# Thinner spacing of a copy beside a chain of matrix units, earlier first loads, and a shorter mixed stage in a four-layer graph network

## The reference, cut to what matters

```
x = layernorm(x + L0(x, edges, W1, b1, W2, b2))      # two matrices, then D^-1/2 (A + I) D^-1/2
x = layernorm(x + L1(x, edges, edge_weight, ...))    # two weighted graph convolutions, hidden 128
x = layernorm(x + L2(x, src, dst, W, attn_l, attn_r, bias))   # attention over a node's incoming edges
x = layernorm(x + L3(x, src, dst, edge_attr_32, ...))         # message MLP, segment sum, update MLP
```

## Time and profile before

| what | value |
|---|---|
| median of 3 runs | 3025.3 us (3022.97 to 3028.07) |
| profiled execution, its own time | 3027.55 us |
| its span from first to last instruction | 3025.7 us |
| mean granted TensorE clock | 0.858 |
| busy share PE, DVE, ACT, POOL | 74%, 66%, 46%, 72% |
| moved by DMA | 331.63 MB, 110 GB/s over the span |

### The profile page before, as it was taken

One profiled execution on the slowest core, in us unless ns is written; L12 is line 12 of the kernel. 1 busy time (PEld: TensorE's weight loads), 2 busy tenths in 40 slices (PEclk: granted clock), 3 DMA queues, 4 the chain that ended last, 5 costly groups with the idle time before them and its releaser, 6 DMA issues.

```text
span 3025.7 us, 39571 instructions
## 1 busy us (share of the span) xinstructions
PE 2225.7 (74%) x10732; PEld 1198.3 (40%) x10732; DVE 1987.7 (66%) x3948; ACT 1382.1 (46%) x2555; POOL 2163.7 (72%) x1666
## 2 busy tenths in 40 slices
PE   2788999978888756665688859999365576666665
PEld 1333444434444435454344434444244333333332
DVE  5445788877888868666598966777688443333332
ACT  2666777755554433222344536777232232233322
POOL 7677877778776448887688858888133588888887
PEclk9989999999999979778798969999676587777777
DMA  6998422232655556555344433443366422222221
GB/s 188 290 295 226 95 57 57 57 67 63 133 122 133 123 115 152 133 128 130 76 110 108 115 86 95 102 103 90 89 162 166 98 62 54 55 56 56 56 56 25
DMA packets 619894, 331.63 MB, mean 110 GB/s; under 512 B 535780, under 2 KB 580960, under 8 KB 619677
## 3 DMA queue, kind: packets, MB, share of 16 engines
q1 hardware_dynamic: 546077, 282.42, 36.7%
q0 software_dynamic: 73600, 46.68, 9.1%
HBM read 197.17 MB, written 130.70 MB: 108 GB/s over the span
## 4 chain that ended last, share of the span: by engine, by line
POOL 50%; issue 18%; DVE 9%; DMA 9%; PE 7%; SPq 6%; ACT 1%; DVEq 0%; ACTq 0%; POOLq 0%
POOL g_row L819 34%; POOL x_with_info L826 8%; POOL out_rows L826 7%; DMA x_with_info<-wide 4%; DMA l_b<-t_x 2%; PE bank L1037 2%; SPq L697 2%; PE pair L1017 2%; DVE rT L1651 1%; DMA g_row<-t_x,gidx 1%; PE bank L946 1%; DVE x_r L1628 1%; DVE ss L1574 1%; POOL wide L910 1%; PE pair L946 1%
## 5 line engine op out<-in xcount | busy, mean ns | idle before, releaser
L819 POOL DMA_INDIRECT g_row<-t_x,gidx x600 | 809.5, 1349 | 230.7 <-issue 192.8
L1252 ACT ACTIVATE hid<-pair,b_up 128x1000 f32<-128x1000 f32 x375 | 406.2, 1083 | 44.1 <-PE pair L1018 43.3
L1038 PE MATMUL bank<-hid,w_dn 128*64 128x500 f32 x750 | 418.3, 641 | 0.0
L1037 PE MATMUL bank<-hid,w_dn 128*64 128x500 f32 x750 | 418.3, 641 | 0.0
L1017 PE MATMUL pair<-xT,w_top 64*128 64x500 f32 x550 | 321.5, 666 | 29.3 <-ACT hid L1252 26.9
L819 POOL DMA_INDIRECT g_row<-x_with_info,src_i x200 | 267.9, 1340 | 96.5 <-issue 63.6
L819 POOL DMA_INDIRECT g_row<-in_x,dst_i x200 | 262.7, 1314 | 95.2 <-issue 65.8
L1018 PE MATMUL pair<-xT,w_bot 64*128 64x500 f32 x550 | 322.4, 668 | 0.0
L819 POOL DMA_INDIRECT g_row<-t_h,gidx x200 | 260.9, 1304 | 79.7 <-issue 79.4
L826 POOL DMA_INDIRECT out_rows<-n_r,fidx x200 | 249.6, 1248 | 64.7 <-issue 60.6
L826 POOL DMA_INDIRECT x_with_info<-info_r,sidx x200 | 242.0, 1210 | 60.9 <-issue 60.9
(11 more groups left out here) (259 smaller groups left out, 5266.6 us busy)
## 6 DMA issues: line engine op xcount, KB each, us to landing
x_in<-in_x_cols SPq DMA_DIRECT2D x100, 250.0 KB, 3.1
x_with_info<-wide SPq DMA_DIRECT2D x50, 476.0 KB
wide<-in_x SPq DMA_DIRECT2D x50, 448.0 KB
out_rows<-x_r SPq DMA_DIRECT2D x100, 224.0 KB
l_k<-keep_row SPq DMA_DIRECT2D x150, 125.0 KB
l_a<-t_x SPq DMA_DIRECT2D x150, 112.0 KB
l_k<-on_row SPq DMA_DIRECT2D x50, 250.0 KB
t_x<-x_r SPq DMA_DIRECT2D x100, 112.0 KB
```

The source lines that it names most:

```text
L819: return g.indirect_dma_start(out=to, out_offset=None, in_=table, in_offset=bass.IndirectOffsetOnAxis(ap=index[:, tile:tile + 1], axis=0), ...
L1037: T.matmul(run.down[0:D, 0:CH], w_dn[a.stage][:, 0:D], hid[a.b2][:, 0, :], start=True, stop=True)
L1038: T.matmul(run.down[D:128, 0:CH], w_dn[a.stage][:, 0:D], hid[a.b2][:, 1, :], start=True, stop=True)\
L1252: A.activation(hid[a.b2][:, :, :], run.up[a.b2][:, :, 0:CH], ACT.Relu, bias=b_up[:, a.stage:a.stage + 1]).then_inc(Cn["hid"], 1)
```

## The change

Three things are edited.

1. `ext_in_slot`: behind the slots of MAIN, the remaining 42 steps of the copy stood one per slot (slots 0 to 41). They now stand three per five slots (the first in slot 1, the last in slot 69).
2. The column loads of the first three dense blocks were issued by `ask_for_columns` after all eight early steps, after a wait for DVE's scalars and after three row stores. They are now issued inside the early steps, after the fifth; `ask_for_columns` issues only those from the fourth block on.
3. `DENSE_MIXED` goes from 6 to 4, `BESIDE_D` from 74 to 76, `BESIDE_G` from 15 to 13. By `unit_order` the runs MAIN, WITH_A, WITH_C, WITH_D and WITH_G then have 163, 74, 59, 76 and 13 places. WITH_A loses two units of each dense stage and two empty places, WITH_C gains two units of each stage, WITH_D gains one of stage 1 and one of stage 2, WITH_G loses the same two.

```
-DENSE_MIXED = 6
-BESIDE_D, BESIDE_G = 74, 15
+DENSE_MIXED = 4
+BESIDE_D, BESIDE_G = 76, 13
...
-            return [] if n < 0 else range(min(EXT, EXT_EARLY + n), min(EXT, EXT_EARLY + n + 1))
+            return [] if n < 0 else range(min(EXT, EXT_EARLY + 3 * n // 5), min(EXT, EXT_EARLY + 3 * (n + 1) // 5))
...
             for b in range(EXT_EARLY):
                 ext_step(b)
+                if b == EXT_EARLY - 4:
+                    for first in range(3):
+                        sp.dma_start(x_in_c[first], t["x_cols"][first]).then_inc(Cn[f"in{first}"], 16)
             sp.wait_ge(s_c, C_DINV)
...
                             sp.wait_ge(Cn["res"], DENSE[a.b - 3].at[0] + 1)
-                        sp.dma_start(x_in_c[a.b % 3], t["x_cols"][a.b]).then_inc([Cn["in0"], Cn["in1"], Cn["in2"]][a.b % 3], 16)
+                            sp.dma_start(x_in_c[a.b % 3], t["x_cols"][a.b]).then_inc(Cn[f"in{a.b % 3}"], 16)
```

## The result

The changed kernel takes 2985.18 us (median of 4 runs, 2982.08 to 2987.25), against 3026.69 us for the kernel before in the same series: a ratio of 0.9861 with a 95% interval of 0.9844 to 0.9878, 41.5 us less. The forecast was 49 us less. The profiled execution took 2982.08 us, the fastest of the four, and its span is 2980.3, so between the two profiled spans lie 45.4 us.

The account below looks back on a forecast made before the run. POOL's chain was taken as the bound, with the scatters' start and WITH_A's length deciding ahead of level B. Scatters -28, WITH_A -26, C +3, D +4, G -2 gave -49 us: 2976 us from 3025.3, range 2962 to 2991.

Parts of the forecast that it names:

- The spacing: Copy beside slots 0 to 69: 3.55 us a slot instead of 4.89, scatters at about 332, 28 us earlier.
- (a): Rival before the scatters: the copy's last store is late at 4.1 us a slot, -12 us, 2992 us; chance 0.16.
- (d): Rival in the copy's slots: bytes don't set them, they stay at 4.89 us, 3046 us; chance 0.08 with its surroundings.
- the chain passes an own unit each three slots, 10.7 us, so it stays ahead: Own gathers: POOL takes 13.1 us a block, so its wait on PE, 29.4 us in all, goes.
- The early loads: Start of the chain: first relu at 56 us instead of 63.8, bounds 53.5 and 63.8.
- WITH_A: Units beside the iso gathers: two mixed blocks fewer save 26 us, bounds zero and 41.
- (c): Rival in WITH_A: it is paid by places, not DVE work, -41 instead of -26 us, 2961 us; chance 0.08.
- WITH_C: Beside level C: two more blocks, 18.2 us of DVE work, cost 3 us at the tail; bounds 0 and 18.
- (b): Rival in levels C and D: no usable slack, +18 + 6.4 in place of 3 + 4, about 2993 us; chance 0.13.
- WITH_D: Beside level D: two units more cost 4 us, bounds 0 and 6.4; zero by the weight-load rule.
- WITH_G: Level G: two units fewer save 2 us, bounds 0 and 4.

Follow-up runs that it names:

- z2: The changed kernel with four copy steps per five slots instead of three, the last in slot 52; 2979.7 us, 0.9853 of the kernel before.
- x4: The changed kernel with one copy step per two slots, the last in slot 83 instead of 69; 3026.0 us, 1.0004 of the kernel before.
- x2: The kernel before with only the mixed blocks at four and the runs at 76 and 13 places; 3001.4 us, 0.9927 of the kernel before.
- z4: z3 with SP asking for columns four places ahead instead of seven, in WITH_A alone; 2970.2 us, 0.9823 of the kernel before.
- z3: The changed kernel with 52 dense blocks ahead of the iso blocks, not 49, and three mixed blocks, not four; 2987.2 us, 0.9870 of the kernel before.
- y1: The changed kernel with two mixed blocks instead of four, WITH_A 66 and WITH_C 65 places; 2996.0 us, 0.9904 of the kernel before.
- y4: The changed kernel with 52 dense blocks ahead of the iso blocks, not 49, and one mixed block, not four; 2974.5 us, 0.9831 of the kernel before.

## Why the prediction was right, and where it wasn't

**The spacing.** Right in mechanism and nearly in size: 3.55 us a slot was forecast for the slow stretch and 3.57 measured; the scatters were forecast at 332 and came at 332.57. The 3.55 was a choice a little above what the bytes (3.39) and PE (3.42) gave, so that it was met to 0.02 us is luck; that the bytes set the slot down to about there is shown by z2 and x4. Rivals (a) and (d) fell in the changed kernel, but x4 shows that (a)'s wait for the copy is real one notch further.

What I had wrong is the step "the chain passes an own unit each three slots, 10.7 us, so it stays ahead". An own unit can't pass its own gather. The chain caught up with POOL and from about slot 42 was held to POOL's 13.1 us a block, so unit 70 came at 327.6, not near 305, and the copy's last store came about when POOL's last gather did, not 20 us ahead. Over slots 0 to 69 a slot took 3.91 us, just above the 3.86 from which, by the prediction's own sum, the copy is late. The term survived by luck, because the two ends happened to meet. That POOL's pace and not the 3.55 set the scatters is shown by z2, whose slots took 4.30 us and whose scatters start at 331.3.

**The early loads.** The first relu came at 54.2 (56 forecast). What I didn't say is that POOL's pace makes this worthless: alone they gave 4 us, beside the spacing nothing.

**WITH_A.** 22.4 us in the profile of the change and 25 in x2, against 26 forecast. With six mixed blocks it took 411.1 to 413.8 us in four profiles, with four, behind the same 49 dense blocks, 386.2 to 391.2 in five; the means differ by 24. DVE's busy time there fell from 347.3 to 331.4 us between unit 163 and the last one, 15.9 of the 22.4. I take the rest for idle time that left with the two empty places, which no run shows by itself. Rival (c), by places, is out. But DVE's work is not the whole of it, as the prediction had it: z4 takes 17.8 us from z3's WITH_A with the same units, by SP's queue alone, a term that the prediction didn't have. So what two mixed blocks are worth is not a constant: y1, with two fewer than the change, took 386.7 us, and z3 and y4 show the same waits on SP.

**WITH_C.** Right: DVE went from 220.4 to 230.2 of 240 us, its waits for gathers in the stretch fell from 14.6 to 2.7 us, and only the tail grew, by 1.8 us (3 forecast; 3 also by the means of six profiles each). What rival (b) said of C came true six places later, in y1. The Trainium skill (Perfetto Trace Analysis, Identifying the Most-Contended Engine) takes occupancy as a fair measure for the vector engine; the trace agrees: at 96% the next units had to wait.

**WITH_D.** 4 us were charged. D's gathers took 323.8 us instead of 322.8, with PE busy 232.5 and its weight loads 109 of 240 us, and the wait from there to G's first product 47.6 instead of 45.3. From D's first gather to G's first product the five profiles with 74 places took 365.4 to 370.4 us and the nine with 76 took 368.0 to 372.7; the means differ by 2. The Trainium skill (Perfetto Trace Analysis, Identifying the Most-Contended Engine) has PE's room judged by its weight loads and not by its matmul busy time. By that the prediction came to zero; the traces lie halfway between zero and the 4 charged, and decide for neither.

**WITH_G.** The term of -2 us was read from one delay of 1.3 us in a stage whose length differs by 4 us from one execution to the next with the same units. In the pair of profiles G got 3 us longer. The term's range should have been that spread.

The sum was 49 us; the profiles differ by 45.4 and the medians by 41.5. In the profiles the first iso unit comes 28.3 us earlier (28 forecast), WITH_A is 22.4 us shorter (26), and what follows gives back 5.3 (5). That the last two agree is luck: POOL's wait ahead of B is 5.6 us longer, B's gathers are 3.7 shorter, and neither stood in the forecast. The further 3.9 us between profiles and medians are within the spread of the runs, the changed kernel's profile being that of its fastest.

## What to carry to other kernels

When work is thinned out beside a chain that shares its queue, compute both ends: when the chain is freed, and when the thinned work itself is done; a spacing with slack on the second cost nothing here (z2), and one without it cost the gain of the whole change (x4). A chain that is made faster runs until it meets its next supplier, so find that supplier's rate before you extrapolate the chain's. And when units are moved between stages, look at the in-order queue that serves them: a request issued ahead for one buffer can hold up stores that another engine waits for, and asking later was worth some 14 us here (z4 against z3).

## What the runs showed that I had not expected

With the DMA engines busy 100% of a stretch, they moved 275 GB/s, 279 at 98% in z2, and 283 at 98% before. Level C's lag on DVE is invisible in POOL's gathers and comes out whole at the end of the level, as 18.6, 23.4 and 38.7 us of wait for 50, 59 and 65 places beside it.
